# A graph kernel's sort: counts and bases of all chunks ahead of its columns, moments on VectorE, code bits on GpSimd, a bias product of 128 rows

## What is computed

```
h   = relu(layernorm(x))
x   = x + segment_sum(relu(concat(h[src], h[dst]) @ W0.T + b0), src)
h   = relu(layernorm(x))
msg = (h @ W1.T)[src] * edge_weight
out = segment_sum(msg, dst)
x   = x + where(out >= 0, out, alpha * out)
```

## Time and profile before

| | us |
|---|---|
| median of 3 runs | 1008.88 |
| lowest and highest run | 1006.73, 1010.54 |
| the profiled execution | 1017.97 |
| its span | 1016.2 |

### The profile page before, as it was taken

The page is one execution under the profiler, slowest core; times in us unless marked ns, Lnnn a source line. Parts: engine busy times, 40 slices in busy tenths (PEclk is TensorE's granted clock), DMA queues, the critical chain, the costliest instruction groups (busy, mean ns, idle before and its releaser), DMA issues.

```text
span 1016.2 us, 20178 instructions
## 1 busy us (share of the span) xinstructions
PE 972.9 (96%) x4719; PEld 781.0 (77%) x4720; DVE 872.2 (86%) x1747; ACT 775.0 (76%) x1650; POOL 643.0 (63%) x934
## 2 busy tenths in 40 slices
PE   5799999999799999999999999999999999999998
PEld 5477778787678887788878778878888788778776
DVE  6989988897769999999999999999999888873444
ACT  4887878778788888888888888888888776755210
POOL 2478877767477777777777777777777755530000
PEclk9689999899989999999999999999999999999999
DMA  8000000000021111111111111111111100010011
GB/s 220 4 3 4 2 4 2 4 2 3 19 62 42 44 42 41 40 42 43 41 43 42 40 40 41 43 42 41 44 41 42 31 30 30 24 42 1 21 41 40
DMA packets 35923, 35.16 MB, mean 35 GB/s; under 512 B 7778, under 2 KB 32095, under 8 KB 35876
## 3 DMA queue, kind: packets, MB, share of 16 engines
q1 hardware_dynamic: 31176, 33.95, 10.7%
q0 software_dynamic: 4416, 0.30, 1.7%
q10 hardware_dynamic: 284, 0.33, 0.1%
HBM read 30.92 MB, written 3.29 MB: 34 GB/s over the span
## 4 chain that ended last, share of the span: by engine, by line
PE 68%; DVE 2%; ACT 1%; issue 1%; POOL 0%; POOLq 0%
PE node_ps L1166 8%; PE edge_ps L1205 8%; PE edge_ps L1211 8%; PE edge_ps L1210 8%; PE edge_ps L1206 8%; PE node_ps L1167 8%; PE m_ps L1177 4%; PE psum L1309 3%; PE psum L1311 3%; PE psum L1310 3%; PE m_ps L1291 1%; PE edge_ps L1269 1%; PE edge_ps L1270 1%; PE edge_ps L1261 1%; PE edge_ps L1266 1%; PE edge_ps L1265 1%
## 5 line engine op out<-in xcount | busy, mean ns | idle before, releaser
L1398 ACT ACTIVATE msg_hi<-edge_ps 128x512 fp32r<-128x512 f32 x332 | 197.6, 595 | 60.8 <-PE edge_ps L1211 60.7
L1122 POOL TENSOR_TENSOR M<-M,pair_w 125x125 f32 x332 | 160.7, 484 | 126.9 <-DVE pair_w L1545 97.2
L1559 DVE SCALAR_TENSOR_TENSOR msg_lo<-edge_ps,msg_hi 128x512 fp32r<-128x512 f32 x332 | 223.6, 683 | 17.3 <-ACT msg_hi L1398 13.0
L417 POOL DMA_INDIRECT edge_table<-fields,row_no x136 | 170.4, 1253 | 58.2 <-issue 47.4
L844 ACT ACTIVATE lane_piece<-hot_lane,fields 125x128 fp32r<-125x128 bf16 x498 | 153.8, 392 | 12.1 <-DVE hot_lane L504 11.8
L705 PE MATMUL psum<-hot_tile,lane_piece 125*128 125x384 f32 x582 | 145.8, 373 | 9.2 <-ACT lane_piece L844 6.3
L1106 POOL TENSOR_TENSOR hot_w<-hot_d,weight_l 128x252 fp32r<-128x252 bf16 x166 | 140.0, 843 | 0.0
L1166 PE MATMUL node_ps<-msg_hi,hot_s 128*125 128x512 f32 x332 | 135.1, 407 | 0.0
L1205 PE MATMUL edge_ps<-b_hi,turned_d 125*128 x332 | 132.7, 400 | 0.7 <-ACT turned_d L1382 0.7
L1211 PE MATMUL edge_ps<-a_lo,turned_s 125*128 x332 | 131.9, 397 | 0.0
L1210 PE MATMUL edge_ps<-a_hi,turned_s 125*128 x332 | 131.4, 396 | 0.2 <-ACT turned_s L1382 0.2
(11 more groups left out here) (258 smaller groups left out, 2044.8 us busy)
## 6 DMA issues: line engine op xcount, KB each, us to landing
spread<-edge_rows SPq DMA_DIRECT2D x190, 125.0 KB
out_dram<-result SPq DMA_DIRECT2D x10, 224.0 KB
edge_table<-fields,row_no POOLq DMA_INDIRECT x136
w_in<-in_L_gnn_W_dram SPq DMA_DIRECT2D x1, 2048.0 KB, 12.7
S<-in_x_dram SPq DMA_DIRECT2D x1, 1792.0 KB
w_in<-in_L_gnn_W_dram SPq DMA_DIRECT2D x1, 1024.0 KB, 5.1
S<-in_x_dram SPq DMA_DIRECT2D x1, 448.0 KB
edge_table<-zeros SPq DMA_DIRECT2D x1, 384.0 KB, 14.9
```

The source lines that it names most:

```text
L417: pool.indirect_dma_start(table_dram[:, :], bass.IndirectOffsetOnAxis(ap=row_no[:, c:c + 1], axis=0), fields[:, c, 0:TABLE_FIELDS], None). ...
L1122: pool.tensor_tensor(part, part, pair_w[h][:, j, 0, 0:BN], ALU.add).then_inc(m_added, 1)
L1398: act.activation(msg_hi[j][:], edge_ps[j][:], ACT.Relu).then_inc(hi_ready, 1)
L1559: dve.scalar_tensor_tensor(out=msg_lo[j][:], in0=edge_ps[j][:], scalar=0.0, in1=msg_hi[j][:].bitcast(F32), op0=ALU.max, op1=ALU.subtract). ...
```

## The change

- PE counts all five chunks ahead of the columns, in five pairs of PSUM banks of which some are used twice, and `counts` in the columns goes. ACT copies each chunk's counts into a tile of its own; SP moves them.
- DVE runs two scans instead of five: one for chunk 0, and one over the other 264 columns at column 4 of chunk 0. SP's row DMAs for chunk k then wait for the picks of chunk k-1.
- SP loads the second part of x (blocks 2 to 9) behind all counts; W0 is loaded from ACT's queue, and the zeros of the table from POOL's.
- The eight steps of the four pairs of weights (turns and low parts, 16 in all) stand one by one behind the 15 prefixes of chunk 0.
- The moments are DVE's `bn_stats` and `bn_aggr`; per block ACT takes a square root (`deviation`) and DVE a reciprocal and the shift. Block 0 stands ahead of the columns, block b at columns 2, 3, 11 and 12 of the 16 of block b-1. ACT loads the table of the square root at its start.
- The code bits, five instructions of DVE, become nine of POOL, which start when `mix_no` is made.
- `ones_r` and `bias_r` have 128 rows; all but two are zero.

```diff
-                        if part == 0:
-                            sp.dma_start(w_in[:], w0.rearrange("(o p) i -> p o i", p=P)).then_inc(w_loaded, 16)
...
+                    load_x(0)
...
+                    def rows_of_bases(k):
+                        for r, part in enumerate((base_hi, base_lo)):
+                            sp.wait_ge(base_rows, 2 * min(k, 1) + r + 1)
+                            if k > 0 and r == 0:
+                                sp.wait_ge(picked, k * NPICK)
+                            sp.dma_start(hot[EROWS + r:EROWS + r + 1], part[:, k * CHUNK:(k + 1) * CHUNK]).then_inc(rows_in, 16)
 
                     counts_by_bucket(0)
...
+                    counts_by_bucket(1)
+                    rows_of_bases(0)
+                    sp.wait_ge(upper_row, 1)
+                    sp.dma_start(hot[EROWS + 2:EROWS + 3], base_up[:]).then_inc(upper_in, 16)
+                    for k in range(2, NCHUNK):
+                        counts_by_bucket(k)
+                    load_x(1)
+                    for k in range(1, NCHUNK):
+                        rows_of_bases(k)
...
-                    pool.tensor_copy(ones_r[:], ones[0:2, :]).then_inc(ones_row_r, 1)
...
+                    pool.tensor_copy(ones_r[:], first_two[:]).then_inc(ones_row_r, 1)
+                    own(pool.tensor_copy(bias_r[:], zeros.rearrange("p t f -> p (t f)")[:, 0:D]))
...
+                    pool.wait_ge(pairs_ready, 1)
+                    pair_of, part, upper_bits = blk_a[:, 1, :], local[:, 1, :], local[:, 0, :]
+                    own(pool.tensor_scalar(part, node_f[:, 0, :], float(TILE), None, ALU.mult))
+                    own(pool.tensor_tensor(upper_bits, part, node_f[:, 1, :], ALU.add))
+                    own(pool.tensor_scalar(part, blk[:, 0, :], -float(BN * TILE), None, ALU.mult))
+                    own(pool.tensor_tensor(upper_bits, part, upper_bits, ALU.add))
...
-                    def bases(k):
...
+                    def bases(part):
+
+                        first, last = (0, CHUNK) if part == 0 else (CHUNK, ECOLS)
...
+                    def moment(b, stage):
+
+                        if stage == 0:
+                            dve.wait_ge(x_in[0 if b < X_PARTS[0].stop else 1], 32)
+                            dve.bn_stats(stats[:, b, :], S[0:BN, b, :]).then_inc(moments, 1)
+                            return
+                        dve.wait_ge(moments, 4 * b + stage)
+                        if stage == 1:
+                            dve.bn_aggr(mv[:, b, :], stats[:, b, :]).then_inc(moments, 1)
+                        if stage == 2:
+                            dve.wait_ge(std_ready, b + 1)
+                            dve.reciprocal(rstd[0:BN, b:b + 1], std[:, b:b + 1]).then_inc(moments, 1)
...
-                    own(dve.scalar_tensor_tensor(out=upper_bits, in0=node_f[:, 0, :], scalar=float(TILE), in1=node_f[:, 1, :],
-                                                 op0=ALU.mult, op1=ALU.add))
...
+                            b, stage = divmod(q + STEP, STEP)
+                            if 0 < b < NBLK and stage in MOMENTS_AT:
+                                moment(b, MOMENTS_AT.index(stage))
...
-                                if i == BASES_AT:
-                                    bases(k + 1)
+                                if k == 0 and i == BASES_AT:
+                                    bases(1)
...
+                    for k in range(1, NCHUNK):
+                        count(k)
...
+                    pe.wait_ge(count_out, 3)
                     for g in range(NPICK):
                         prefix(0, g)
-                    weights(2)
-                    weights(3)
+                        weights_part(g)
+                    weights_part(NPICK)
...
-                            if k + 2 < NCHUNK and 0 <= part < 3:
-                                count(k + 2, range(CHUNK // 3 * part, CHUNK // 3 * (part + 1)))
...
+                    act.dma_start(w_in[:], w0.rearrange("(o p) i -> p o i", p=P)).then_inc(w_loaded, 16)
+                    act.wait_ge(dconst, 1)
+                    act.activation(std[:, 0:1], eps_t[0:BN, :], ACT.Sqrt)
...
+                    def deviation(b):
+                        act.wait_ge(moments, 4 * b + 2)
+                        act.activation(std[:, b:b + 1], mv[:, b, 1:2], ACT.Sqrt, bias=eps_t[0:BN, :]).then_inc(std_ready, 1)
...
-                    moments(range(2))
...
+                    for k in range(3):
+                        copy_counts(k)
...
+                    deviation(0)
+                    for pair in range(KC):
+                        turned_weights(pair)
```

More of the change, by code:

```diff
@@ L209, in build @@
             minus_ident = sb1("minus_ident", [P, P], F32R)
-            ones_r = sb1("ones_r", [2, P], F32R)
+            ones_r = sb1("ones_r", [P, P], F32R)
             before_b = sb1("before_b", [P, P], BF16)
[L212 to L218, removed]
+            counts = sb1("counts", [NBKT, ECOLS], BF16)
+            running = sb1("running", [NBKT, ECOLS + 1], F32)
+            base_hi = sb1("base_hi", [NBKT, ECOLS], BF16)
+            base_lo = sb1("base_lo", [NBKT, ECOLS], BF16)
+            mix_at = sb1("mix_at", [NBKT, 1], F32)
             planes = sb1("planes", [EROWS, 2 * PICK, CHUNK], F32)
@@ L319, in _, with load_x @@
                         sp.dma_start(src_i[rows], src.rearrange("(p c) -> p c", p=EROWS)[rows]).then_inc(src_in, 16)
[L320 removed]
+                    def load_x(part):
                         for rows in SPLIT:
[L322 to L324 removed]
+                            sp.dma_start(S[rows, X_PARTS[part]],
+                                         x.rearrange("(b p) d -> p b d", p=BN)[rows, X_PARTS[part]]).then_inc(x_in[part], 16)
@@ L331, in counts_by_bucket @@
                     def counts_by_bucket(k):
                         sp.wait_ge(count_out, k + 1)
-                        if k > 0:
-                            sp.wait_ge(scan_step, k)
-                        sp.dma_start(counts[:, 2:CHUNK + 2], counts_out[:]).then_inc(counts_in, 16)
-                    counts_by_bucket(0)
[L338 to L346, removed]
+                        sp.dma_start(counts[:, k * CHUNK:(k + 1) * CHUNK], counts_out[:, k]).then_inc(counts_in[min(k, 1)], 16)
@@ L670, in _, with count @@
                 def _(pe):
-                    def count(k, cols):
-                        for c in cols:
-                            if c == 0 and k > 1:
-                                pe.wait_ge(picked, k * NPICK)
+                    def count(k):
+                        if k > 2:
+                            pe.wait_ge(count_out, k - 2)
+                        for c in range(CHUNK):
                             at = k * CHUNK + c
@@ L722, in low_w, with weights_part @@
                                   skip_group_check=True).then_inc(w_low, 1)
-                    def weights(pair):
-                        for i in (2 * pair, 2 * pair + 1):
-                            turn_w(i)
-                        for i in (2 * pair, 2 * pair + 1):
-                            low_w(i)
+                    def weights_part(n):
+                        pair, part = divmod(n, 4)
+                        (turn_w, turn_w, low_w, low_w)[part](2 * pair + part % 2)
                     def turn_h(b):
```

151 lines of the change are left out of this document (60 added, 91 removed).

## The result

Medians: **1013.03 us** (15 runs, 1010.55 to 1015.25) against 1009.62 for the kernel before (15 runs, 1006.42 to 1012.43). The ratio is **1.0034, with a 95% interval of 1.0021 to 1.0046**: 3.4 us slower, inside what the prediction called no change, but on the other side of zero from the forecast 1007.7.

The account below looks back on a forecast made before the run. PE was taken as busiest before, DVE as bounding the columns after. First column +8.2, chunk 0 -1.9, chunks 1 to 3 -7.0, tail -0.5, together -1.2: 1016.8 profiled, 1007.7 median, no change; range 998 to 1017.

Parts of the forecast that it names:

- the subtraction: Whole kernel: terms together -1.2 against the profiled 1017.97, so 1016.8; carried to the median 1008.88, so 1007.7.
- chunk 0 -1.9: First chunk's columns: 42.0 against 43.87, with DVE as the bound, 40.9 busy and 1.1 idle.
- chunks 1 to 3 -7.0: Columns of these chunks: 134.1 against 141.07, with DVE 129.7 busy and 4.4 idle.
- Code bits on POOL: Front: nine POOL instructions beside DVE's chain delay it by 1.0, ends none and 4.2.
- Rival 3: Front: each of nine POOL instructions holds DVE's chain for half to all of 1.05; 1013.8 us, chance 0.06.
- Counts' transfer: Front: counts land ahead of DVE's base table, its 4.24 wait goes, first prefix 4.3 earlier at 25.4.
- Weights between prefixes: Front: prefixes with eight weight turns of 1.72 and low parts take 19.5 (18.1 to 22.5); first column 8.2 later.
- Scatters "take that up": POOL's scatters start as much later as the front, but their 10.9 us of waiting for `slots` absorbs it.
- Moments: Columns: DVE gains 1.2 per block, two blocks in chunk 0, seven in chunks 1 to 3, none in the tail.
- counts and bases: Out of the columns: PE loses 5.7, DVE 2.4 with 0.5 added on the remaining scan, ACT a 3.04 stall.
- bias: Bias product of 128 rows on PE: 0.30 saved per block, 3.0 for ten, bound below 0.
- Rivals 1 and 2: Columns: first, PE was the bound, 999.8 us, chance 0.30; second, DVE becomes the bound, 1017.7 us, chance 0.16.

Follow-up runs that it names:

- before_again: The kernel before with no edit, profiled a second time: 1008.74 us.
- code_on_vector: The changed kernel with the code bits back on DVE, behind the tables of chunk 0: 1009.23 us, ratio 1.0000 to the kernel before.
- code_late: The changed kernel with the code bits on POOL held back until DVE has cast chunk 0's bases: 1009.09 us, ratio 0.9990 to the kernel before.
- moments_out: The changed kernel without the moments of blocks 1 to 9, all normalised with block 0's: 1013.48 us, ratio 1.0038 to the kernel before.

## Why the prediction was wrong

- **The step that failed is the subtraction.** The changed kernel itself was forecast 3 too long, not too short: first tile at 51.0 (49.27 came), chunk 0 42.0 (39.87), chunks 1 to 3 134.1 (135.09), the profile 1016.8 (1013.64). It was set against the one profile of before, 9.1 above its median, and the difference was then carried over to the median. That profile's extra lay in the very stretches that were to shrink. Against `before_again`, "chunk 0 -1.9" and "chunks 1 to 3 -7.0" measured +1.9 and -3.1. With DVE busy 37.46 of 38.02, chunk 0 had nothing to give, and two blocks of moments lengthen it.
- **Code bits on POOL (+1.0, ends 0 to 4.2) was mis-sized.** The hold is 4.0 on the timeline and 3.4 to 4.4 in the time (`code_on_vector`, `code_late`), the upper end or a little past it. Nine POOL instructions lie beside that stretch, six of the code bits (2.4, 0.40 each) and the three of the weight behind them (1.6), which the prediction didn't count. So the 0.46 of the earlier trace rows was near the price; what failed is taking a tenth of it because the row's median is near its minimum, which tells at most how often a sum of that loop was held, and not what a chain loses that runs beside POOL without a break. Rival 3, which is the one that the sentence on SBUF means, is what happened in kind, though its holds of 4.7 to 9.5 are above the 4.0; 0.06 was too little for it. That its 1013.8 lies so near the time is luck in part, as it rests on the same subtraction. The test that was named, a first prefix past 29, read it rightly.
- **Counts' transfer (4.3 earlier) was right**: with the hold gone the prefix starts at 25.49, 25.4 forecast.
- **Weights between prefixes (19.5) was too long**, 14.5: only the first two turns took 1.7, the later ones 0.9 to 1.0. The turn's price came from the earlier trace rows at 17.80, where it is 1.72; `before_again` shows its second pair, from 23.27, at about half that. This and the small hold cancelled in part: first tile +8.2 forecast, +5.2 measured. Prefixes and turns in less than 15 together was a sign of being wrong that the prediction had named. What makes a turn cost the one or the other is open: the granted clock reads 1.00 from 30 to 47 in the changed kernel, for both kinds.
- **Scatters "take that up" was wrong.** The 10.9 of waiting for `slots` belonged to the first profile; in `before_again` they wait for it once, for 0.3, so there was nothing to take the delay up. They also end, with the table's read, within 2.6 us of the last column. A later first slot moves them one for one: in the profiles of the two kernels without moments 3.2 at the start make 2.9 at the end. The ratios of these two differ by 5.4, more than this chain explains; the rest is open.
- **Moments (1.2 per block)** measured 1.27 in length but 0.93 in DVE's busy time. In chunk 0 DVE is the bound, as forecast: 2.1 less busy makes it 2.1 shorter (`moments_out`). In chunks 1 to 3 neither engine alone is: 6.2 less on DVE shorten them by 2.9, and with **counts and bases** back 6.1 more on PE and 0.9 on DVE lengthen them by 4.3, and the time by 3.4; the **bias** is worth 1.6 to 1.8 of 3.0. So there a microsecond of either engine counts for about a half. Rivals 1 and 2 each took one of the two for the bound. The range, 998 to 1017, held the time because it reached to both.
- The **bias product** does what the row showed, 0.30 per block, and not 0.

The parts together: the change's gains in the columns are real and small; two ways in which it was put at the front, the time of POOL's work and the weights between the prefixes, cost 6.4 and turn a kernel of 1006.5 into one of 1013.0. The moments off ACT, the second part of x behind the counts and the other queues for W0 and the zeros were not tried by themselves.

## What to carry to other kernels

When the one profile lies far from the median, take a second before any difference is formed, or predict the changed kernel's stages and compare with busy times, which differ less than lengths. Work moved to an idle engine is not free by itself: ask what the other engines do at that time. Here the same POOL instructions cost 4 us beside a DVE chain of 0.2 us steps and nothing that shows some microseconds later. Before shortening a stage, follow every chain that ends it, also the one that shows no waits.

## What was not expected of the hardware

Here a product over 2 rows among products over 128 is not slow in its load. TensorE's lines for the bias product of `before_again` and of the changed kernel (min/median/max in ns):

```profile
L750 PEld LDWEIGHTS psum<-bias_r,ones_r x10: 178/178/179, 61.2 to 234.0; 2*125 2x125 f32 x10
```
```profile
L777 PEld LDWEIGHTS psum<-bias_r,ones_r x10: 185/186/328, 66.7 to 237.7; 128*125 128x125 f32 x10
```

So the Trainium skill's rule that a load goes by columns ("TensorE: Matmul & The Clock Gate", section "LDWEIGHTS (loading the stationary operand)") holds for the load, 178 against 186 ns. What costs is a gap ahead of it, and ahead of the load of the next product, which the groups of loads of `before_again` show, about 0.25 us each time (the last column is idle time and what ended it):

```profile
L751 PEld LDWEIGHTS psum<-w0T_hi,h1T_hi 128*125 128x125 f32 x80 | 15.0, 188 | 2.4 <-issue 2.4
L750 PEld LDWEIGHTS psum<-bias_r,ones_r 2*125 2x125 f32 x10 | 1.8, 178 | 2.5 <-issue 2.5
```

The gap is gone when the bias product has 128 rows. Not every change in the number of rows brings it: the loads of 125 rows (`lane_piece`) and of 128 rows (`h1T_hi`) that follow each other in `before_again`, as at 100.99 and 101.56, have no idle time between them. Its mechanism wasn't tried.
